# Two stacked Mamba blocks: intermediate results moved by fewer, larger DMAs, and 11 multiplications moved from VectorE to GpSimd

## The reference: what is computed

```python
xz = u @ W_in;  xr, z = split(xz)
x = silu(causal_conv(xr) + conv_b)                 # 192 inner channels, 4 taps
dt, B, C = split(x @ W_x)                          # 6 + 16 + 16 columns: the "x_proj" results
delta = softplus(dt @ W_dt + b_dt)
h[t] = exp(delta[t] * A[n]) * h[t-1] + (delta*x)[t] * B[n, t]      # for 16 states n
y[t] = sum_n h[t, n] * C[n, t]  + x * D;   out = (y * silu(z)) @ W_out
```

## Time and profile before

| | |
|---|---|
| runs shown, us | 8181.68, 2150.37, 2139.63: median 2150.37 |
| the profiled execution, us | 2146.87 |
| its span, first to last instruction, us | 2144.7 |
| mean granted TensorE clock | 0.947 |
| POOL busy | 1914.5 us, 89% |
| PE busy | 1867.0 us, 87% |
| DVE busy | 1815.2 us, 85% |
| ACT busy | 1153.9 us, 54% |
| DMA | 416.22 MB, mean 194 GB/s |

### The profile page before, as it was taken

How to read it: one execution, slowest core, us unless ns; L and a number is a source line. 1 busy time by engine, 2 the same in 40 slices (tenths; PEclk the granted TensorE clock), 3 DMA queues, 4 the chain that set the end, 5 groups by cost and what they waited for, 6 DMA issues and landing times. The chain is left out here.

```text
span 2144.7 us, 17077 instructions
## 1 busy us (share of the span) xinstructions
PE 1867.0 (87%) x4966; PEld 691.2 (32%) x4966; DVE 1815.2 (85%) x1083; ACT 1153.9 (54%) x1182; POOL 1914.5 (89%) x842
## 2 busy tenths in 40 slices
PE   6797889798898799889889789879979988978777
PEld 2332333233243233233333233323323323322222
DVE  1888897677888988997798997898889989799994
ACT  3666465556656445644665645735565564453331
POOL 0998899896998998998799899899799999989995
PEclk8899999899999999999899989999999999999897
DMA  3667658555675765785676686676566576668673
GB/s 98 224 208 166 202 191 208 164 189 169 170 241 195 193 207 185 203 238 172 181 210 217 188 207 198 218 192 222 178 167 214 180 216 205 217 183 225 222 220 82
DMA packets 126249, 416.22 MB, mean 194 GB/s; under 512 B 20092, under 2 KB 24460, under 8 KB 126156
## 3 DMA queue, kind: packets, MB, share of 16 engines
q1 hardware_dynamic: 126012, 415.06, 64.3%
q10 hardware_dynamic: 144, 0.07, 0.0%
HBM read 404.63 MB, written 6.29 MB: 192 GB/s over the span
## 5 line engine op out<-in xcount | busy, mean ns | idle before, releaser
L898 POOL TENSOR_TENSOR ring<-ring,c_ring 128x1024 f32<-128x1024 f32 x576 | 1347.0, 2366 | 154.7 <-DMA c_ring<-c_rows 79.6
L511 PE MATMUL y_ps<-ring,wp 128*128 128x512 f32 x2304 | 1173.3, 626 | 46.9 <-DVE yv_fwd L828 18.7
L848 DVE TENSOR_TENSOR_SCAN ring<-a_ring,b_ps 128x1024 f32<-128x1024 f32 x390 | 891.5, 2286 | 32.3 <-issue 0.5
L511 PEld LDWEIGHTS y_ps<-ring,wp 128*128 128x128 f32 x2304 | 432.4, 197 | 569.1 <-issue 459.1
L848 DVE TENSOR_TENSOR_SCAN ring<-b_ps,b_ring 128x1024 f32<-128x1024 f32 x186 | 422.1, 2276 | 79.9 <-POOL b_ring L892 47.2
L495 PE MATMUL b_ps<-b_in,sel 96*64 96x512 bf16 (+1 forms) x1076 | 250.5, 406 | 177.5 <-DVE ring L848 174.3
L811 DVE TENSOR_TENSOR b_ps<-u_ab,b_ps 128x1024 f32<-128x1024 f32 x242 | 293.7, 1214 | 104.9 <-PE b_ps L495 90.4
L651 ACT ACTIVATE a_ring<-delta_ab,wp 128x1024 f32<-128x1024 f32 x242 | 273.9, 1140 | 186.4 <-DVE ring L848 178.5
L892 POOL TENSOR_TENSOR b_ring<-u_ab,b_ring 128x1024 f32<-128x1024 f32 x142 | 335.7, 2364 | 4.9 <-DMA b_ring<-b_rows 4.9
L644 ACT ACT_TABLE_LOAD x186 | 238.6, 1283 | 74.6 <-DVE ring L848 33.1
L651 ACT ACTIVATE b_ps<-delta_ab,wp 128x1024 f32<-128x1024 f32 x142 | 158.4, 1117 | 215.1 <-DVE ring L848 214.0
(11 more groups left out here) (83 smaller groups left out, 815.2 us busy)
## 6 DMA issues: line engine op xcount, KB each, us to landing
c_ring<-c_rows SPq DMA_DIRECT2D x384, 512.0 KB, 4.6
c_ring<-c_rows SPq DMA_DIRECT2D x384, 256.0 KB, 4.4
b_ring<-b_rows SPq DMA_DIRECT2D x142, 512.0 KB, 5.4
b_ring<-b_rows SPq DMA_DIRECT2D x88, 256.0 KB, 5.5
out<-io SPq DMA_DIRECT2D x16, 192.0 KB, 3.6
io<-x SPq DMA_DIRECT2D x6, 384.0 KB, 5.8
b_in<-parts SPq DMA_DIRECT2D x72, 32.0 KB, 1.8
dt_in<-parts SPq DMA_DIRECT2D x138, 12.0 KB
```

Source lines behind the costliest of these rows:

```text
L511: nc.tensor.matmul(half(y_ps[:, :], j), ident, half(ring[:, g % RING, :], j), start=(n == 0 and kind != ROWS), stop=(n == NS - 1)).then_in ...
L848: nc.vector.tensor_tensor_scan(out=h, data0=a, data1=b, initial=0.0, op0=ALU.mult, op1=ALU.add).then_inc(h_ready, 1)
L898: nc.gpsimd.tensor_tensor(r, r, c_ring[:, g % C_RING, :], ALU.mult).then_inc(g_ready, 1)
```

## The change: what it does

1. The B and C rows share one tensor in HBM, `bc_rows`, and one in SBUF, `bc_out`: 2 DMAs in place of 4.
2. `DT_TERMS` is in another order, so that a gather can take all needed parts of a row at once: 3 DMAs per half (36, 24 and 12 destination rows) in place of 6. The rows of the weights and of the selecting matrix are packed to match.
3. `b_in` is filled by one DMA per half in place of 3. With points 1 and 2 the code issues 2 + 6 + 2 = 10 DMAs per item where it had 22.
4. A third-tile row is spread by one DMA in place of two. Its source is a pattern of 2 images x 64 readings x 1024 numbers, its destination 128 partitions.
5. `BY_POOL` has 197 POOL steps in place of 186, and some slots of the plan's tables move by 0.5 to 2.

```diff
-DT_TERMS = ((0, 0), (0, 1), (1, 0), (1, 1), (0, 2), (2, 0))
+DT_TERMS = ((0, 0), (1, 0), (2, 0), (0, 1), (1, 1), (0, 2))
+DT_RUNS = ((0, 3), (3, 2), (5, 1))
...
-           2: (2, 5, 8, 9, 11, 14, 16, 18, 19, 22, 23, 31, 39, 42),
+           2: (2, 4, 8, 9, 11, 12, 13, 14, 16, 17, 18, 19, 20, 22, 23, 25, 31, 39, 42),
...
-            for q, (g, _) in enumerate(DT_TERMS):
-                eng.dma_start(half(dt_in[2 * RANK * q:2 * RANK * (q + 1), :], h),
-                              parts3[C_AT * h + B_ROWS:C_AT * h + SPLIT_ROWS, g, :]).then_inc(K["dt_loaded"][kind], 16)
+            rows = parts3[C_AT * h + B_ROWS:C_AT * h + SPLIT_ROWS, :, :]
+            for q, n in DT_RUNS:
+                eng.dma_start(half(dt_in[2 * RANK * q:2 * RANK * (q + n), :], h),
+                              rows[:, 0:n, :]).then_inc(K["dt_loaded"][kind], 16)
...
-                        sp.dma_start(half(b_rows[slot].rearrange("b n t -> (b n) t"), h),
-                                     b_out[C_AT * h:C_AT * h + B_ROWS, :]).then_inc(c_kept, 16)
-                        sp.dma_start(half(c_rows[slot].rearrange("b n t -> (b n) t"), h),
-                                     c_out[C_AT * h:C_AT * h + B_ROWS, :]).then_inc(c_kept, 16)
+                        to = bc_rows[slot].rearrange("v b n t -> (b n) v t")[:, :, h * HALF:(h + 1) * HALF]
+                        sp.dma_start(to, bc_out[C_AT * h:C_AT * h + B_ROWS, :, :]).then_inc(c_kept, 16)
...
-                        for g in range(3):
-                            sp.dma_start(half(b_in[B_ROWS * g:B_ROWS * (g + 1), slot, :], h),
-                                         parts3[C_AT * h:C_AT * h + B_ROWS, g, :]).then_inc(K["bc_loaded"][kind], 16)
+                        sp.dma_start(half(b_in[:, slot, :], h), parts3[C_AT * h:C_AT * h + B_ROWS, :, :]).then_inc(K["bc_loaded"][kind], 16)
...
             def spread_row(dst, rows, k, n, landed_in):
-                if k < 2:
-                    sp.dma_start(dst, rows[k, n:n + 1, :].to_broadcast([P, T])).then_inc(landed_in, 16)
-                    return
-                for b in range(2):
-                    sp.dma_start(dst[b * DM:(b + 1) * DM, :],
-                                 rows[b, n:n + 1, :].to_broadcast([DM, T])).then_inc(landed_in, 16)
+                src = rows[k, n:n + 1, :].to_broadcast([P, T]) if k < 2 else rows[:, n:n + 1, :].to_broadcast([2, DM, T])
+                sp.dma_start(dst, src).then_inc(landed_in, 16)
```

More of the change, by code:

```diff
@@ L39 @@
 B_LEAD = 6
-BY_POOL = {0: (0, 2, 6, 9, 10, 12, 16, 19, 21, 23, 26, 29, 30, 34, 38, 43),
[3 rows of a table removed]
[L44 to L48, removed]
+BY_POOL = {0: (2, 6, 7, 10, 12, 16, 19, 21, 23, 25, 29, 30, 34, 39, 43, 45),
[3 rows of a table added]
+           ROWS: (2, 4, 6, 10, 12, 17, 19, 20, 23, 25, 30, 31, 34, 38, 46),
+           FWD: (1, 2, 4, 7, 8, 9, 10, 14, 16, 17, 18, 21, 22, 25, 30, 38, 41, 42),
+           BWD: (1, 2, 6, 7, 10, 16, 17, 21, 22, 25, 31, 35, 37, 43, 44, 47),
+           10: (5, 8, 9, 14, 16, 17, 19, 20, 22, 25, 30, 31, 40, 44),
+           11: (1, 2, 6, 8, 10, 16, 17, 20, 24, 25, 31, 33, 35, 40, 41, 44)}
 _cols, _at = {}, 0
@@ L320, in build_program @@
         dve_before = [g - n for g, n in enumerate(pool_before)]
[L321 to L329, removed]
+        c_uses = [16 * (g // C_RING + 1) for g in range(ALL_STEPS)]
+        b_uses = {g: 16 * (m // B_RING + 1) for m, g in enumerate(pool_steps)}
         b_slot = lambda g: pool_before[g] % B_RING
@@ L457, in look_ahead_c @@
                 if g % STEPS == 0:
-                    sp.wait_ge(c_kept, 64 * (g // STEPS + 1))
+                    sp.wait_ge(c_kept, 32 * (g // STEPS + 1))
                 wait(sp, g_ready, g - C_RING + 1)
-                spread_row(c_ring[:, g % C_RING, :], c_rows[parity(kind, pair)], k, n, c_spread[g % C_RING])
+                spread_row(c_ring[:, g % C_RING, :], bc_rows[parity(kind, pair), 1], k, n, c_spread[g % C_RING])
             def look_ahead_b(g):
@@ L471, in look_ahead_b @@
                         sp.wait_ge(h_ready, pool_steps[m - B_RING] + 1)
-                    spread_row(b_ring[:, b_slot(g), :], b_rows[parity(kind, pair)], k, n, b_spread[b_slot(g)])
+                    spread_row(b_ring[:, b_slot(g), :], bc_rows[parity(kind, pair), 0], k, n, b_spread[b_slot(g)])
             walk(SP_ORDER, job, SP_LEAD, ahead_b=look_ahead_b, ahead_c=look_ahead_c)
@@ L704, in job @@
                     src = full(unit)
-                    nc.scalar.activation(b_out[:, :], src, ACT.Copy).then_inc(K["b_cut"][kind], 1)
+                    nc.scalar.activation(bc_out[:, 0, :], src, ACT.Copy).then_inc(K["b_cut"][kind], 1)
                     nc.scalar.activation(parts3[:, 0, :], src, ACT.Copy).then_inc(K["hi_ready"][kind], 1)
                 elif name == "dbl":
-                    empty(unit, nc.scalar.activation(c_out[:, :], full(unit), ACT.Copy))
+                    empty(unit, nc.scalar.activation(bc_out[:, 1, :], full(unit), ACT.Copy))
                 elif name == "constants":
@@ L934, in pack, with put @@
     wp = np.zeros((P, NCOL), np.float32)
-    def put(name, layer, a, row=0, at=0):
+    def put(name, layer, a, row=0, at=0, step=1):
         c = _cols[name, layer][0] + at
-        wp[row:row + a.shape[0], c:c + a.shape[1]] = a
+        wp[row:row + step * a.shape[0]:step, c:c + a.shape[1]] = a
     for layer, pre in enumerate(("L0_conv_", "L1_conv_")):
@@ L952, in pack @@
                 put("w_dbl", layer, w[P:], b * DM, 2 * X_COLS + at)
-            for q in range(len(DT_TERMS)):
-                put("w_dt", layer, w_dt[:, :P], RANK * (2 * q + b), b * P)
-                put("w_dt", layer, w_dt[:, P:], RANK * (2 * q + b), 2 * P + b * DM)
+            for first, n in DT_RUNS:
+                for q in range(n):
+                    row = 2 * RANK * first + RANK * b * n + q
+                    put("w_dt", layer, w_dt[:, :P], row, b * P, n)
+                    put("w_dt", layer, w_dt[:, P:], row, 2 * P + b * DM, n)
         put("w_out", layer, w_out[:P])
@@ L970, in pack @@
             for n in range(NS):
-                sel[(g * 2 + b) * NS + n, b, n] = 1.0
+                sel[3 * (b * NS + n) + g, b, n] = 1.0
     split = np.zeros((DT_ROWS, 2), np.float32)
-    for q, (_, g) in enumerate(DT_TERMS):
-        split[2 * RANK * q:2 * RANK * (q + 1)] = (-1.0 if g >= 1 else 0.0, -1.0 if g == 2 else 0.0)
+    for first, n in DT_RUNS:
+        for q in range(n):
+            g = DT_TERMS[first + q][1]
+            split[2 * RANK * first + q:2 * RANK * (first + n):n] = (-1.0 if g >= 1 else 0.0, -1.0 if g == 2 else 0.0)
     put("centre", None, np.eye(C, dtype=np.float32) - np.full((C, C), 1.0 / C, np.float32))
```

24 lines of the change are left out of this document (11 added, 13 removed), and 4 rows, old and new, of the table BY_POOL.

## The result

The changed kernel took 3790.44 us (median of 4 runs, 3785.02 to 3792.09) against 2149.24 us before (median of 4): ratio 1.7658, 95% interval 1.7596 to 1.772. The ratio leaves out the run of 8181.68 us, which no other run of this kernel resembles. The forecast was 3720 us, range 3500 to 4000. The profiled execution took 3792.09 us, its span 3788.6 us.

A forecast was written before the change was run, and what follows sets the result against it. It took POOL, busy 1914.5 of 2144.7 us, as the bound, with SP's issue time at `bc_in` stalling it. Profiled time plus terms: 2146.9 + 1671 - 65 + 21 - 52 = 3722, so 3720 us, range 3500 to 4000.

The forecast's parts named there:

- The count of end marks: Packets under 512 B, one per engine a DMA uses: 2 engines per third-tile row would give 11144, 16 engines 14476.
- the fixed pair: In third tiles, all one-DMA rows use the same two engines and queue: 238 x 10.2 = 2428 us; chance 0.82.
- The price of a row: A third-tile row on 2 engines, 262144 B each, was to take 9.9 to 10.8 us, taken as 10.2.
- The third-tile stretches: The 12 stretches needing third-tile rows, product 28 to 47, were to grow from 761.8 to 2433 us, +1671.
- 53 - 48 = 5: Third-tile stretches beside the rows: 53 us for landing and last product, -48 for B rows issued early.
- The rest: The 11 stretches between third tiles, 1198.1 us, were to take 1102 us for 1043 us of POOL work.
- the -52 for work ahead: While starving in a third tile, POOL would do two u*B of the next item ahead: 11 x 2 x 2.37 us.
- the 11 stalls: POOL's 11 waits for a C row at `bc_in`, 79.6 us; outside third tiles the change was to save 65.
- The merged DMAs at `bc_in`: 10 DMAs issued instead of 22, 7.9 us less SP issue time per item: -65 us, or -73 in the rival.
- the table: 11 more u*B on POOL: 26 us there, 21 outside third tiles; DVE relieved of 13 us.
- All 16 engines: Rival: the third-tile row's DMA runs on all 16 engines, giving 2087 us, 2.8% faster; chance 0.10.
- the run's mean of 18.8 GB/s per engine: Mean engine rate over the whole run, giving 13.9 us per third-tile row; left outside the price as counting overlapping packets twice.

The follow-up runs named there:

- experiment 9: The changed kernel with each third-tile row taken from one image only, by one DMA on 16 engines (does not compute the reference): 2064.16 us, ratio 0.9625.
- experiments 5 and 7: 5: kernel before, each third-tile half row's DMA with first dimension 4, 2690.29 us. 7: changed kernel, third-tile B rows in two DMAs, 3468.39 us.
- experiment 1: The changed kernel with only the third-tile row undone, spread by two DMAs again: 2064.10 us, ratio 0.9623.
- experiment 2: The kernel before with only the third-tile row spread by one DMA, everything else as before: 3841.77 us.

## Why the prediction was right

**The count of end marks** carried the forecast, and it held in each kernel to the packet (11144, 18284, 13012, 14428, 16316, and 14476 in experiment 9). Before the change ran, the rule that the first dimension, and not the number of pieces, sets the engines stood on 4 packets of 20092, those of one load; the experiments with 2, 4 and 8 in front now bear it out. The two engines are shown by the changed kernel's own rows, and the fixed pair by experiments 5 and 7.

**The price of a row** was taken as 10.2 us from 9.9 to 10.8; it was 10.165 us.

**The third-tile stretches** were to take 2433 us and took 2496.7. The rows are 238 x 10.165 = 2419, so the ends of the stretches add 77 us where I had 53 - 48 = 5. That term was mis-sized. I had let the next item's first rows pass beside the pair. They go over 16 engines, but the pair is among them. POOL in time at the end of the third item's third tile:

```profile
987.96 2.34 POOL L883 TENSOR_TENSOR ring<-ring,c_ring 128x1024 f32<-128x1024 f32 x1 [8.83 <-DMA c_ring<-bc_rows]
...
999.51 2.34 POOL L883 TENSOR_TENSOR ring<-ring,c_ring 128x1024 f32<-128x1024 f32 x1 [6.92 <-DMA c_ring<-bc_rows]
...
1012.42 6.95 POOL L883 TENSOR_TENSOR ring<-ring,c_ring 128x1024 f32<-128x1024 f32 x3 [8.27 <-DMA c_ring<-bc_rows]
```

The last products are 11.5 and 12.9 us apart, not 10.2: between two third-tile rows stand one or two 128-row spreads of the next item, 8 packets or 1.3 us each on the pair. Some five of them per item (three C rows and the B rows of up to six steps ahead) are 6.5 us, 72 in 11 items, about the 72 missing. Over all 12 stretches the distances between rows run over 10.165 us by 67 us in all, mostly at the end of a third tile and some at its start. That is read from spacing and order, and was not tested apart.

**The rest** was to take 1102 us and took 1113.2, but that is luck: two of its terms were wrong, by 52 and 43 us, and nearly cancel. The first is the -52 for work ahead. POOL does its work in program order, and these stretches begin and end at products, so no u*B can pass from one kind of stretch to the other because POOL starves. The kernel of experiment 1 has the same order on POOL, no starving, and as much POOL work between third tiles, 1092.0 us against the changed kernel's 1091.5 where I forecast 1043:

```profile
sum 1128.83, PE 1042.64 PEld 397.36 DVE 983.61 ACT 666.41 POOL 1091.98; mean PE 94.79 PEld 36.12 DVE 89.42 ACT 60.58 POOL 99.27
```

So the term is nothing. In its place POOL's waits for scans between third tiles fell from 61.3 to 18.3 us, which I had left as they were. In experiment 1, with the same table, 32.0 us of them are left. The last 14 went because DVE did work ahead in the long third tiles: it was busy for 925.0 us between them, against 983.6 in experiment 1, and for longer within them (781.4 against 711.9). C-row waits there fell from 59.7 to 1.9 us, 58 where I had 65: two of the 11 stalls lie in third tiles, 10.1 and 9.8 us long, and not one. With 1.7 us less of waits for B rows and 17.4 us more of POOL work, 1198.1 - 57.8 - 43.0 - 1.7 + 17.4 = 1113.0 us.

Over the whole kernel the gains were split wrongly too. The merged DMAs at `bc_in` are worth 59.6 us, not 65 to 73, and the table wins 19.7 where I charged 21, or 26 - 13 in the rival. For the rival *All 16 engines* this is why its 2087 us proved to be 2064.

**One argument was wrong, without harm.** I put the run's mean of 18.8 GB/s per engine aside since "packets of several DMAs overlap and are counted twice". They hardly do: with all engines busy the packet times add up to 104% of them, no more. The DMA views of the kernel before, of 10 us in a third tile and of 2 us in another one:

```profile
DMA packets 694, 2.27 MB, mean 227 GB/s; under 512 B 141, under 2 KB 141, under 8 KB 694
...
q1 hardware_dynamic: 694, 2.27, 104.3%
```

```profile
DMA packets 239, 0.85 MB, mean 424 GB/s; under 512 B 32, under 2 KB 32, under 8 KB 239
...
q1 hardware_dynamic: 239, 0.85, 103.8%
```

All 16 engines are busy in both. In the first, 553 data packets took 1.043 x 16 x 10 / 553 = 0.30 us each; in the second 207 took 0.16. The mean was low in large part because two 64-row DMAs really move at about half the rate of a 128-row one. Had that held for the new row too, a row would have taken 64 x 0.30 = 19 us and the kernel some 5900. So nothing that I gave ruled out slow packets for the new row; the price of 10.2 us, and with it the upper end of the range, came true without a reason for it.

## What to carry to other kernels

Before DMAs are merged, write down the first dimension of each side's pattern as issued: the end marks (packets under 512 B) tell how many engines each DMA gets, and a first dimension of 2 on one side got two here, for 512 KB. Merging paid where it kept 12 or 32 in front and shortened a queue that the bottleneck waited behind (22 issues to 10, 2.8%). Where it put 2 in front, alone, it made the kernel 1.79 times as long (experiment 2). A step moved to the busiest engine can still win, if it fills time in which that engine waits. An engine that starves does nothing of its own ahead of its program order; it is the engines upstream that get ahead.

## What the runs showed of the hardware that I had not expected

**Spreads over 64 partitions.** With 16 engines, 4 KB packets of 64-row spreads take 0.30 us and those of 128-row spreads 0.16; 227 against 424 GB/s. With 8 engines the 64-row packets take 0.26, with 4 engines 0.16, and so do those of the new row on 2. The Trainium skill (SBUF — State Buffer, "Door 1: The DMA port swizzle") states that partitions 0 to 63 reach only 8 of the 16 ports, and 64 to 127 only the other 8. With 16 engines on 8 ports, two to a port would follow, and packets twice as long. The trace fits that with its 0.30 against 0.16, and with 4 engines; the 0.26 with 8 engines it leaves unexplained. Which port a packet took no row shows, and no run tests another cause.

**SP is held when few engines carry much.** An issue of 0.32 us took 9.96 us in the third tiles of the changed kernel, and 17.0 at most. SP in time, start and duration in us:

```profile
3594.29 9.96 SPq L436 DMA_DIRECT2D b_ring<-bc_rows  x1
3604.30 9.96 SPq L436 DMA_DIRECT2D c_ring<-bc_rows  x1
3614.31 9.97 SPq L436 DMA_DIRECT2D b_ring<-bc_rows  x1
```

The seven issues from 3584.28 us on took 71.3 us, 10.2 each, the pace of the rows. My reading is that only a few such rows fit into the queue, and an issue ends when there is room for it. In the steady part it cost nothing by itself, since the pair never ran dry, but everything else in SP's queue waits behind it.

**The clock.** The mean granted TensorE clock fell from 0.947 to 0.734, with 0.69 in the first third tile shown above and 0.57 to 0.67 in the others: PE waited for POOL's products, which waited for rows. In 25 us of such a third tile, with PE busy for 7.6 us, it was granted 0.50 throughout, the 1.2 GHz level of its two:

```profile
3595.00:3620.00 25.00, 7.56 (x8) 2.35 (x8) 3.50 (x2) 3.23 (x3) 6.49 (x3) 0.50 0.13 52
```

PE's y_ps matmuls grew from 626 to 746 ns on the mean. DVE waited longer for PE (357.4 us for `b_ps`, 115.7 before), but POOL waited for PE in no row, and its rows came at the pace of the two DMA engines. Between third tiles the clock was back at 0.91 to 0.98.
